# Tokens written to regions of their experts in three groups, beside attention and beside the tiles

## The reference

```python
    def _L0_ffn_ref(x, router_w, up_proj, down_proj):
        E = 8; H = 256; D = 256; TOP_K = 2
        xt = x.reshape(-1, H)                              # 2048 tokens
        logits = jnp.einsum('nh,eh->ne', xt, router_w)
        probs = jax.nn.softmax(logits, axis=-1)
        scores, expert_idx = jax.lax.top_k(probs, TOP_K)
        scores = scores / jnp.sum(scores, axis=-1, keepdims=True)
        gate = jnp.zeros((N, E), dtype=xt.dtype).at[jnp.arange(N)[:, None], expert_idx].add(scores)
        h = jnp.einsum('nh,ehd->end', xt, up_proj)
        hidden = jax.nn.silu(h[..., :D]) * h[..., D:]
        out_e = jnp.einsum('end,edh->enh', hidden, down_proj)
        out = jnp.einsum('ne,enh->nh', gate, out_e)
...
    x = _layernorm(x + _L0_attn_ref(x, L0_attn_Wk, L0_attn_Wv, L0_attn_Wo, L0_attn_freqs), axis=-1)
    x = _layernorm(x + _L0_xattn_ref(x, ctx_1024, ctx_1024), axis=-1)
    x = _layernorm(x + _L0_ffn_ref(x, L0_ffn_router_w, L0_ffn_up_proj, L0_ffn_down_proj), axis=-1)
```

## Time and profile before

| | |
|---|---|
| median of 3 runs | 262.21 us (262.04 to 262.63) |
| profiled execution | 263.22 us, of which the span from first to last instruction is 261.4 us |
| PE busy | 207.2 us (79% of the span) |
| DVE, ACT, POOL busy | 161.7, 111.1, 146.5 us |
| mean granted clock of TensorE | 0.929 of full |
| moved by DMA | 35.75 MB |

### The profile page before, as it was taken

How to read it: one execution, slowest core, us unless ns; L and a number is a source line. 1 busy time by engine, 2 the same in 40 slices (tenths; PEclk the granted TensorE clock), 3 DMA queues, 4 the chain that set the end, 5 groups by cost and what they waited for, 6 DMA issues and landing times.

```text
span 261.4 us, 5197 instructions
## 1 busy us (share of the span) xinstructions
PE 207.2 (79%) x1365; PEld 182.3 (70%) x1366; DVE 161.7 (62%) x534; ACT 111.1 (42%) x277; POOL 146.5 (56%) x156
## 2 busy tenths in 40 slices
PE   8578999999999997756999999999999999300000
PEld 8467798898998896745888988888888888200000
DVE  4765888889887684954454544454545454017993
ACT  2233144244234113541454545454545555425665
POOL 0064775676666410565576777777777774415340
PEclk9999999999999999979999999999999999955555
DMA  7962674775671012801222323233232341089323
GB/s 196 384 228 67 251 230 144 270 222 151 230 240 45 0 44 82 280 3 60 80 93 89 100 85 100 88 99 100 85 100 88 102 97 61 11 263 327 134 88 153
DMA packets 20130, 35.75 MB, mean 137 GB/s; under 512 B 2861, under 2 KB 11312, under 8 KB 20112
## 3 DMA queue, kind: packets, MB, share of 16 engines
q1 hardware_dynamic: 16368, 26.21, 30.1%
q0 software_dynamic: 3744, 9.31, 11.7%
HBM read 27.12 MB, written 9.31 MB: 139 GB/s over the span
## 4 chain that ended last, share of the span: by engine, by line
PE 63%; DVE 16%; DMA 6%; POOL 5%; issue 5%; ACT 2%; SPq 1%; DVEq 1%; ACTq 0%; POOLq 0%
PE p_c L545 14%; PE p_v L545 7%; PE p_y L467 5%; PE p_v L411 4%; PE p_y L571 4%; PE p_r L545 4%; PE p_c L427 4%; PE p_a L545 3%; PE p_s L545 3%; PE p_t L584 3%; POOL space L999 3%; PE p_s L451 3%; DVE space L838 3%; PE p_a L486 2%; PE p_r L495 2%
## 5 line engine op out<-in xcount | busy, mean ns | idle before, releaser
L545 PE MATMUL p_c<-w_hi,parts 128*128 x104 | 34.6, 414 | 0.0
L1023 POOL DMA_INDIRECT y_dram<-x1T,scatter_now x26 | 26.3, 1013 | 11.9 <-issue 6.5
L1003 POOL DMA_INDIRECT turns<-x_dram,gather_now x26 | 25.5, 979 | 12.6 <-issue 3.8
L969 POOL TENSOR_TENSOR w_lo<-keep,w_hi 128x384 fp32r<-128x384 f32 (+1 forms) x32 | 31.3, 999 | 0.0
L981 POOL TENSOR_TENSOR space<-back 128x512 f32<-128x512 f32 x8 | 10.1, 1268 | 30.9 <-DVE back L704 30.9
L810 DVE TENSOR_TENSOR parts<-p_y,parts 128x256 fp32r<-128x256 f32 x39 | 16.5, 423 | 17.7 <-ACT parts L912 17.7
L820 DVE TENSOR_TENSOR cs<-p_c,cs 128x256 f32<-128x256 f32 x26 | 11.0, 424 | 22.7 <-ACT cs L919 22.7
L919 ACT ACTIVATE cs<-p_c 128x256 f32<-128x256 f32 x26 | 10.0, 385 | 24.7 <-PE p_c L545 24.7
L545 PEld LDWEIGHTS p_c<-w_hi,parts 128*128 128x128 f32 x104 | 17.6, 189 | 2.3
L1034 POOL TENSOR_TENSOR space<-space,keep 128x512 f32<-128x512 f32 (+1 forms) x8 | 10.4, 1298 | 15.0 <-ACT space L941 15.0
L912 ACT ACTIVATE parts<-p_y 128x256 fp32r<-128x256 f32 x39 | 14.8, 380 | 8.8 <-PE p_y L571 8.6
(11 more groups left out here) (153 smaller groups left out, 552.0 us busy)
## 6 DMA issues: line engine op xcount, KB each, us to landing
keep<-in_weights SPq DMA_DIRECT2D x8, 768.0 KB, 4.8
space<-y_dram SPq DMA_DIRECT2D x16, 256.0 KB, 4.0
space<-in_xT SPq DMA_DIRECT2D x8, 256.0 KB, 3.1
keep<-in_x SPq DMA_DIRECT2D x8, 256.0 KB, 2.8
space<-in_ctxT SPq DMA_DIRECT2D x8, 256.0 KB, 5.2
space<-in_ctxt SPq DMA_DIRECT2D x8, 256.0 KB, 4.9
x_dram<-x SPq DMA_DIRECT2D x8, 256.0 KB, 4.7
keep<-x_dram SPq DMA_DIRECT2D x1, 2048.0 KB, 8.2
```

What stands on the lines that cost most here:

```text
L545: last = nc.tensor.matmul(dst, lhs[:, k, :], w[:].rearrange("p e n -> p (e n)")[:, bass.ds(start + col + k * width, width)], start=(n == 0 ...
L969: return nc.gpsimd.tensor_tensor(w_lo[:, bass.ds(e, 1), :].rearrange("p a n -> p (a n)")[:, n], w_in[s][:, n], whole[:, n].bitcast(F32), A ...
L1003: nc.gpsimd.indirect_dma_start(xs[s], None, x2_dram, bass.IndirectOffsetOnAxis(ap=gather_now[s][:], axis=0)).then_inc(xs_ok[s], 16)
L1023: nc.gpsimd.indirect_dma_start(y_dram, bass.IndirectOffsetOnAxis(ap=scatter_now[s][:], axis=0), ys[s], None, bounds_check=TOPK * N - 1, oo ...
```

## The change

- Each expert gets a region of 17 x 128 rows in DRAM (`rows_dram`, REGION = 17); x2 stays in SBUF (`x2_rows`, with two words behind each row: where its result goes, and which expert was the first choice). x2 is no longer saved and reloaded.
- Blocks are routed in three groups: 0 to 7, 8 to 11, 12 to 15. For a group g DVE runs `choose(g, 0)`, `choose(g, 1)`, `mark(g)`; PE counts (`place(g)`); DVE makes the row of each token in its region (`destinations(g)`); POOL sends the rows of each block once for each choice by an indirect DMA (`send`): 16, 8 and 8 of them. DVE then lists which tiles are full (`count_tiles(g)`, `list_tiles(g)`, and `pass_over(g)` between lists). The three lists hold 9, 8 and 22 tiles, 39 in all.
- Group 0 is chosen in step 6 of attention, its rows are sent in steps 7 (six sends) and 8 (ten). Groups 1 and 2 are routed between the tiles: DVE at tile steps -1 to 4 and 6 to 8, POOL's sends of group 1 in tile steps 1 to 4 and of group 2 in 7 to 10, two a step.
- A tile is 128 consecutive rows of a region and SP loads it by a plain DMA whose row number is read into a register (`load_tile`, four buffers). Ahead of the first tile of a list it waits for all sends of the group; ahead of tile 17 it also writes 128 zero rows behind the end of each region (eight register reads and eight DMAs), and waits for them.
- The address of a put is worked out by DVE from the two extra words (`put_idx`). y lies in DRAM with both choices of a token side by side, so that a pair comes back in one load of 512 KB.
- The loops over tiles and over PE's steps are written out; p_down has two buffers instead of three; exp and the gates are worked out behind the last tile.

```diff
-DVE_ROWS, POOL_ROWS, ACT_ROWS = range(0, 11), range(11, 20), range(20, TOPK * B)
+REGION = TOPK * N // 2 // P + 1
+GROUPS = ((0, 8), (8, 12), (12, B))
+PHASES = []
+for first, end in GROUPS[:-1]:
+    PHASES.append(-(-(TOPK * P * end - E * (P - 1)) // P) - sum(PHASES))
+PHASES.append(TILES - sum(PHASES))
...
@@ SP
-            sp.dma_start(x2_keep.rearrange("p j n -> p (j n)").rearrange("p (j q d) -> p (j q) d", q=2, d=D),
-                         x2_dram.rearrange("(j t) d -> t j d", t=T)).then_inc(x2_back, 16)
+            def load_tile(k):
+                g, kk = phase_of[k], in_phase[k]
+                if k >= XS:
+                    sp.wait_ge(xt_ok, k - XS + 1)
+                    sp.wait_ge(put_idx_ok, k - XS + 1)
+                if kk == 0:
+                    sp.wait_ge(table_ok, g + 1)
+                    sp.wait_ge(rows_ok[g], 16 * TOPK * (GROUPS[g][1] - GROUPS[g][0]))
+                    if g == 0:
+                        sp.wait_ge(lo_ok, PAIRS)
+                    if g == 2:
+                        for e in range(E):
+                            at = sp.value_load(fill_idx[0:1, e:e + 1], min_val=0, max_val=E * REGION * P)
+                            sp.dma_start(rows_dram[bass.ds(at, P), :], fill[:]).then_inc(filled, 16)
+                        sp.wait_ge(null_ok, 16)
+                        sp.wait_ge(filled, 16 * E)
+                at = sp.value_load(row_idx[g][0:1, kk:kk + 1], min_val=0, max_val=E * REGION * P)
+                sp.dma_start(xs[k % XS], rows_dram[bass.ds(at, P), :]).then_inc(xs_ok[k % XS], 16)
...
@@ DVE, tile step
+                if k == -1:
+                    choose(1, 1)
+                    mark(1)
+                if k == 0:
+                    destinations(1)
+                if k == 1:
+                    pass_over(0)
+                    count_tiles(1)
+                if k == 2:
+                    list_tiles(1)
...
@@ POOL
+            def send(g, blocks):
+
+                pool.wait_ge(dest_ok, g + 1)
+                for b in blocks:
+                    for c in range(TOPK):
+                        nc.gpsimd.indirect_dma_start(
+                            rows_dram, bass.IndirectOffsetOnAxis(ap=dest_idx[:, c, b:b + 1], axis=0),
+                            x2_rows[:, b, :], None, bounds_check=E * REGION * P - 1, oob_is_err=False).then_inc(rows_ok[g], 16)
...
+                if isinstance(i, int) and i == PAIRS - 1:
+                    pool.wait_ge(dest_in, 1)
+                    send(0, (0, 1, 2))
+                if isinstance(i, int) and i == PAIRS:
+                    send(0, (3, 4, 5, 6, 7))
...
-            def tile(k, at, has):
-                if has(4):
-                    s, _ = at(1)
-                    pool.wait_ge(gather_now_ok, k + 5)
-                    pool.sem_inc(carried, 1)
-                    gather(s)
+            def tile(k, has):
...
+                if k in (1, 2, 3, 4):
+                    send(1, (k + 7,))
+                if k in (7, 8, 9, 10):
+                    send(2, (k + 5,))
```

## The result

| | median | runs | profiled execution | span | mean clock |
|---|---|---|---|---|---|
| before | 262.12 us (262.02 to 262.63) | 4 | 263.22 us | 261.4 us | 0.929 |
| changed | 285.21 us (284.19 to 288.57) | 4 | 286.16 us | 284.4 us | 0.870 |

The changed kernel takes 1.086 times as long (95% interval 1.081 to 1.092): **slower by 23.1 us** by the medians, 22.7 by the ratio. I had forecast 7.6 us and a range up to 278.0.

What follows compares the result with a forecast made beforehand. PE was taken to bound the kernel (63% of the chain), with DVE also full in attention. Terms: -0.2 us at T(1), carried to +8.3 at T(38), -0.7 behind, +7.6 in all: 269.8 us, range 260.0 to 278.0.

Steps and rivals of the forecast that it cites:

- a send at 1.28 us: On POOL, each indirect DMA of 128 rows was priced like a put, 1.28 us from one to the next.
- cs at 93.6 and 111.3: On POOL, cs of pairs 6 and 7, behind the sends, start at 92.8 and 110.7 instead of 82.61 and 92.27.
- T(9): Start on PE of the transposes of tile 9, first of the second list: 145.4 against 141.99, with a 2 us gap.
- T(17): Start on PE of tile 17's transposes, first of the third list: 171.8 against 162.77, gap 5 to 6 us.
- a finish 0.6 us shorter: Behind the last tile, one 512 KB load a pair halves SP's 16 issues: -0.7 us, bounds -3 and +1.
- the +1 us for the clock ahead of T(0): After idling in steps 7 and 8, PE returns at 1.2 GHz; p_a, fillers and transposes run slower: +1 us.
- T(0): T(k) is the start of tile k's transposes on PE; T(0) forecast at 119.7 us against 121.21 before.
- the 0.75 us for each read and write in SP's list: Ahead of tile 17 on SP, eight zero-row writes, each a register read and an issue: 8 x 0.75 = 6.0 us.
- T(38): Start on PE of the last tile's transposes: 225.1 us against 216.82, 8.3 us later.
- T(1): Start on PE of tile 1's transposes: 122.4 us against 122.64, so the front wins 0.2 us.
- the put of tile 0: On POOL among the sends of group 1, due at 129.6 us, once ACT has copied tile 0's down product.
- the last send of group 2: On POOL ahead of tile 17, puts and sends end at 159.9 us and the last send lands at 161.1.

Runs made afterwards that it cites:

- e2: Changed kernel without the 15 filler matmul calls of step 9 on PE: 283.12 us, ratio 1.078.
- e4: Changed kernel with 24 and 21 more filler calls on PE in the waits for cs of steps 7 and 8: 284.02 us, ratio 1.081.
- e5: e4 with fillers also ahead of the transposes of tile 9 (9 calls) and tile 17 (38 calls): 281.58 us, ratio 1.076.
- e1: Changed kernel with cs ahead of the sends of group 0 on POOL in steps 7 and 8: 281.57 us, ratio 1.069.
- e10: Changed kernel with the edits of e1, e2 and e3 together, groups as in the change: 269.17 us, ratio 1.018.
- e12: e10 with the last expert's w_lo made by DVE in four pieces instead of by POOL in step 8: 265.69 us, ratio 1.012.
- e3: Changed kernel with SP's eight zero-row writes moved from ahead of tile 17 to behind the loads of tiles 12 to 15: 274.37 us, ratio 1.044.
- e6: e1 with groups of 6, 6 and 4 blocks instead of 8, 4 and 4: 287.45 us, ratio 1.098.
- e9: e8 with one send ahead of cs in step 7, DVE's w_lo in four pieces behind destinations(1), and fewer fillers before tile 0: 260.14 us, ratio 0.990.
- e8: e1 and e3 together, group 1 routed in attention, group 2 chosen before the tiles, last w_lo on DVE, fillers before tile 0: 262.02 us, ratio 0.996.
- e11: e9 with more matmul fillers on PE in the two waits of step 9: 261.00 us, ratio 0.993.

## Why the prediction was wrong in size

The direction and most of the mechanism were right: a send at 1.28 us, cs at 93.6 and 111.3 (92.8 and 110.7 forecast), a wait at T(9) of 2.0 us (2), one at T(17), though of 8.9 us instead of 5 to 6, a finish 0.6 us shorter (0.7). Two steps failed above all: the +1 us for the clock ahead of T(0), with a path on which PE's transposes wait for DVE and not for fillers, and the 0.75 us for each read and write in SP's list. The error is 15.3 us at T(38), in five terms.

- **"+1 us" for the clock ahead of T(0): +4.8 at T(1).** I saw that PE would idle for 6 us and some 9 us (6.3 and 5.4) and come back at 1.2 GHz, and priced it by feel. p_a took 2.07 us and not 1.13, the logits matmuls 1.71, and the thirty fillers of step 9 6.34 us instead of 3.59, in front of transposes whose input lay ready 4.3 us before. I had counted these fillers as what fills a wait; behind a stall, with the rest of the chain shifted, they are work on the path. e2 and e4 each bring T(0) forward, by 3.2 and 3.7 us. Both act on the same thirty fillers, so the two should not add up; together they were not tried.
- **Up to T(9): +2.1 more.** The first two sends of group 1 are done by 134.1, and then POOL waits 2.35 us: what sets the rest is the put of tile 0, at 136.49 instead of 129.6. T(3) is 0.9 us later behind T(1) than I had it (132.51), and the put comes 4.0 us behind T(3) instead of 2.8. From the last send to T(9) it was 5.6 us, for 5.5 forecast.
- **Up to the last send of group 2: +2.7 more** (168.19 instead of about 158.6). Behind the wait at T(9) the clock was 0.57; T(10) comes after 4.19 us and T(11) after 3.76 instead of 2.54. e5, at full clock there, still needs 6.4 us for the two, so 1.3 us is DVE's, and the remaining 1.6 of 7.95 goes with the clock. The first put behind them waits (2.84 us idle on POOL, until 157.96), and the sends behind the put. (My text has one round of a put and two sends too many there; the 159.9 counts the right number.)
- **Behind T(17): +2.4.** 55.67 us for 21 tiles instead of 53.3, which e5 shows to be the clock.

From 6.9 at T(9): 6.9 + 2.7 + 3.3 + 2.4 = 15.3 us. The low clock is in the first, third and last term: 0.9 of p_a and 2.8 of the fillers, up to 1.6, and 2.4, some 7 to 8 us together, of which I had given 1. The waits of 5.4 us and more are paid once as such and once more as slow work behind them; for the wait of 2.0 us at T(9) this is not shown, as e1, e2, e4, e10 and e12 have it without the low clock. e3 shows how they hang together: its edit takes away 8.9 us of wait and gives 10.8.

**Right about the sign, but not for all reasons.** With groups 1 and 2 routed between the tiles no run won (e10 is at 1.018, e12 at 1.012). e1 shows that even with cs out of the way the sixteen sends set T(0), and e6 that starting still earlier only opens a wait at tile 5. What made the idea pay was to get group 1 out as well before the tiles begin, to keep SP's zero rows off the path, to take w_lo off POOL and to trim the fillers: 1.0%, in e9, where these stand together.

**Not settled:** what sets the last 1 to 2 us between e8, e9 and e11, whose front moves by 4 us while the total moves by 2.

## What to carry to other kernels

Price a long new wait on PE twice: its length, and the work behind it at the lower clock, fillers included (here waits of 5.4 us and more had it, waits of 2 us mostly not); a filler that was free in a wait is on the path as soon as its data comes first. Ask of each list of small DMAs whether its addresses are known earlier, and price a register read with its arithmetic and issue together. When work is cut into groups, the question is not when the first group starts but whether the second is there when the first has run out.

## What the runs showed that I had not expected

**VectorE and GpSimd hold each other.** A pair of DVE TENSOR_SCALAR of 0.74 us took 5.14 us beside POOL's TENSOR_TENSOR of 3.84 us, and a send of 0.97 us took 2.42 beside a DVE TENSOR_TENSOR of 1.76 us with both inputs in SBUF (1.88 us in e12, where it was cut in four pieces, and 1.25 and 1.10 for two sends in e9). In e8 and e12 the send is longer by about what was left of DVE's w_lo when it began, 1.45 us for 1.58 and 0.91 for 1.04; in e9, beside the same four pieces, by much less, and what decides this is open. The trace of before seems to have it in small, which I had passed over: the pair of L651 below ends at 87.83, and w_lo beside it at 87.68.

```profile
86.41 1.42 DVE L651 TENSOR_SCALAR x<-r,mv,rs 128x256 f32<-128x256 f32 x2
```

The Trainium skill (SBUF — State Buffer, Who interferes with whom) states this: the two engines share a pair of ports, and whichever has it keeps it for its whole instruction while the other is blocked; a tensor_scalar in its fast mode and a tensor_tensor with two inputs in SBUF are named as takers. The rows here agree as to who holds whom, and go further in two points. The ports were kept not for one instruction but through all four of w_lo (5.14 us beside 3.84), and for a tensor_tensor the page names only what GpSimd reads and infers that descriptor generation stays free of it, while here a send took 2.42 us beside one. The 0.7 us left open under e12 it does not explain either.

**The clock after a wait.** Behind waits of 5.4 to 8.9 us the granted clock was 0.50 in 92 to 98, 112 to 120 and 180 to 190, the lower of its two levels, and the slow part behind the last one cost 2.65 us (e4 against e5). Behind waits of 1.9 to 2.8 us at T(9) it was 1.00 in five kernels and 0.57 and 0.58 in two.
